# Turning half of the attention probabilities in 32x32 squares on VectorE and through DRAM, in a fused attention and feed-forward kernel

## The reference

```python
scores = jnp.einsum('bhnqd,bhnkd->bhnqk', qb, kwin) * scale
scores = jnp.where(mask[None, None], scores, jnp.float32(-1e+30))
attn = jax.nn.softmax(scores, axis=-1)
out = jnp.einsum('bhnqk,bhnkd->bhnqd', attn, vwin)
...
return out @ Wout + bout
```

## Time and profile before

| | |
|---|---|
| median of 3 runs | 2630.02 us (2627.89 to 2631.48) |
| profiled execution | 2629.41 us |
| its span | 2627.6 us |
| TensorE (PE) matmul, weight load | 98%, 80% of the span |
| VectorE (DVE), ScalarE (ACT), GpSimd (POOL) | 61%, 62%, 24% |
| DMA queues | 167.43 MB, mean 64 GB/s |

### The profile page before, as it was taken

The page is one execution under the profiler, slowest core; times in us unless marked ns, Lnnn a source line. Parts: engine busy times, 40 slices in busy tenths (PEclk is TensorE's granted clock), DMA queues, the critical chain, the costliest instruction groups (busy, mean ns, idle before and its releaser), DMA issues.

```text
span 2627.6 us, 55989 instructions
## 1 busy us (share of the span) xinstructions
PE 2576.2 (98%) x19728; PEld 2090.2 (80%) x19728; DVE 1592.0 (61%) x4779; ACT 1638.1 (62%) x4260; POOL 631.8 (24%) x595
## 2 busy tenths in 40 slices
PE   6999999999999999989999999999999999999998
PEld 4888888888888888868888888888888888888885
DVE  5444444444444444357777777777777777777775
ACT  6333333333333333358888888888888888888886
POOL 0011111111111111033333333333333333333332
PEclk7999999999999999999999999999999999999999
DMA  5422222222222222021121111112111111112110
GB/s 181 146 80 81 80 80 80 80 80 80 80 80 80 80 80 64 33 81 34 34 65 34 53 46 42 58 41 58 34 61 39 42 58 42 58 34 65 34 46 29
DMA packets 188361, 167.43 MB, mean 64 GB/s; under 512 B 11328, under 2 KB 143424, under 8 KB 187632
## 3 DMA queue, kind: packets, MB, share of 16 engines
q1 hardware_dynamic: 188000, 164.41, 20.2%
q0 software_dynamic: 144, 0.17, 0.0%
HBM read 97.43 MB, written 67.11 MB: 63 GB/s over the span
## 4 chain that ended last, share of the span: by engine, by line
PE 55%; ACT 1%; issue 0%; DVE 0%; POOL 0%; POOLq 0%; ACTq 0%
PE pT_ps L1193 14%; PE job_ps L1105 14%; PE score_ps L1176 7%; PE job_ps L1123 7%; PE job_ps L1217 7%; PE job_ps L1114 7%; ACT wqkv_raw L928 1%; ACT wqkv_raw L938 0%; PE job_ps L1237 0%; PE score_ps L1227 0%; DVE wqkv_raw L1006 0%; DVE k_lo L1038 0%; ACT q_hi L954 0%; ACT k_hi L957 0%; POOL wout_raw L899 0%
## 5 line engine op out<-in xcount | busy, mean ns | idle before, releaser
L928 ACT ACTIVATE wqkv_raw<-wqkv_raw,neg_max 128x384 f32<-128x384 f32 (+1 forms) x1024 | 633.3, 619 | 186.3 <-DVE neg_max L1006 181.5
L888 POOL TENSOR_SCALAR wqkv_raw<-wqkv_raw,sum_rcp 128x384 f32<-128x384 f32 (+1 forms) x256 | 372.9, 1457 | 960.1 <-DVE sum_rcp L1017 960.1
L494 ACT ACTIVATE relu<-up_ps,fc_scale 128x512 f32<-128x512 f32 x256 | 176.2, 688 | 656.2 <-PE up_ps L625 656.2
L938 ACT COPY wqkv_raw<-pT_ps 128x384 f32<-128x384 f32 (+1 forms) x1024 | 484.7, 474 | 74.4 <-PE pT_ps L1193 74.1
L1193 PE MATMUL pT_ps<-ident,wqkv_raw 128*128 128x128 f32 x3040 | 513.4, 277 | 8.1 <-ACT wqkv_raw L938 7.7
L1006 DVE CUSTOM_DVE_ANT_0 wqkv_raw<-score_ps,mask 128x384 f32<-128x384 f32 (+1 forms) x1024 | 503.5, 548 | 5.7 <-PE score_ps L1176 1.6
L568 DVE SCALAR_TENSOR_TENSOR sq<-up_ps,relu 128x512 f32<-128x512 f32 x256 | 177.0, 692 | 531.8 <-ACT relu L494 530.4
L1193 PEld LDWEIGHTS pT_ps<-ident,wqkv_raw 128*128 128x128 f32 x3040 | 360.0, 140 | 119.1 <-ACT wqkv_raw L938 42.6
L635 PE MATMUL down_ps<-proj_T,sq_hi 128*128 128x512 f32 x1024 | 408.9, 399 | 0.9 <-DVE sq_lo L551 0.9
L637 PE MATMUL down_ps<-proj_T,sq_lo 128*128 128x512 f32 x1024 | 404.3, 395 | 0.0
L621 PE MATMUL up_ps<-f_xT_hi,fc_T 128*128 128x512 f32 x1024 | 399.2, 390 | 1.4 <-DVE low L539 1.4
(11 more groups left out here) (126 smaller groups left out, 4228.2 us busy)
## 6 DMA issues: line engine op xcount, KB each, us to landing
xT_hi<-xT SPq DMA_DIRECT2D x65, 256.0 KB, 3.8
xT_lo<-xT SPq DMA_DIRECT2D x65, 256.0 KB, 4.5
f_x_in<-in_L_attn_x SPq DMA_DIRECT2D x64, 256.0 KB, 3.2
xT<-f_xT_hi SPq DMA_DIRECT2D x64, 256.0 KB, 2.6
xT<-f_xT_lo SPq DMA_DIRECT2D x64, 256.0 KB, 2.8
part_in<-in_L_attn_x SPq DMA_DIRECT2D x64, 256.0 KB, 3.4
partial<-f_y SPq DMA_DIRECT2D x64, 256.0 KB, 2.0
wout_raw<-partial SPq DMA_DIRECT2D x64, 256.0 KB, 2.8
```

The costliest lines, as they stand in the source:

```text
L888: nc.gpsimd.tensor_scalar(probs[:, u, cols], probs[:, u, cols], sum_rcp[:, u:u + 1], None, ALU.mult).then_inc(last_head_normalised, 1)
L928: nc.scalar.activation(probs[:, u, cols], probs[:, u, cols], ACT.Exp, bias=neg_max[:, u:u + 1], scale=-1.0, accum_out=prob_sum[:, u:u + 1] ...
L938: nc.scalar.copy(pT[:, h, first + seen.start:first + seen.stop, :].rearrange("p w t -> p (w t)"), pT_ps[:, h % 2, seen.start * P:seen.stop ...
```

## The change

Of the two query blocks of a step only block 1 is still turned by TensorE and copied by ScalarE. Block 0 takes another way. VectorE makes one reciprocal for its four heads; heads 0 and 1 are multiplied by ScalarE, head 2 by VectorE, head 3 by GpSimd. VectorE then transposes each head (128x384) in 32x32 squares, in the order 2, 0, 1, 3, into `blocks`. A square stays in its 32 partitions, so the squares must still be moved: SP stores the whole of `blocks` (128 partitions x 12 pieces of 512 B, 786 KB) to a DRAM tensor with one transfer, waits for it, and loads it with four transfers, each into 32 partitions of `pT_moved`. TensorE waits for these four (`blocks_moved`) ahead of the values of step t in step t + 1. These matmuls no longer join both blocks: there are 24 of 128 columns instead of 8 of 256 and 8 of 128. In return for space in SBUF `values` holds 5 blocks instead of 6 and the halves of the result 6 steps instead of 8. SP's list now goes by steps: transfers out and in first, then loads of x (c = 1), then y and `partial` (c = 2 and 3).

The core of the diff (the remaining lines are semaphores, changed counts in waits, and arguments):

```diff
-    VR = 6
+    VR = 5
     XR = 3
+    OR = 6
+    STRIPS = P // DH
...
-        pT = wqkv_raw[:, 2:4, :].rearrange("p a (h w k) -> p (a h) w k", w=6, k=P)
-        oT_hi = sb("oT_hi", [P, 2, DC, T], F32R)
-        oT_lo = sb("oT_lo", [P, 2, DC, T], F32R)
+        blocks = sb("blocks", [P, STRIPS, 3, HC, DH], F32)
+        pT_moved = wqkv_raw[:, 2, :].rearrange("p (w q h t) -> p w q h t", q=STRIPS, h=HC, t=DH)
+        pT = wqkv_raw[:, 3, :].rearrange("p (h w k) -> p h w k", w=3, k=P)
+        oT_hi = sb("oT_hi", [P, OR, T], F32R)
+        oT_lo = sb("oT_lo", [P, OR, T], F32R)
...
+        def transfers_out(steps):
+
+            return steps + (STRIPS - 1) * min(steps, DC)
...
+            def move_blocks_out(t):
+                i, _ = where(t)
+                first = blocks_seen(i, 0).start
+                moved = turned_dram[t % 2 * STRIPS:(t % 2 + 1) * STRIPS, :, :, :]
+                sp.wait_ge(blocks_turned, HC * (t + 1))
+                if first == 0:
+                    sp.dma_start(moved.rearrange("a w p x -> p (a w) x"),
+                                 blocks.rearrange("p a w h t -> p (a w) (h t)")).then_inc(blocks_out, 16)
+                else:
+                    for a in range(STRIPS):
+                        sp.dma_start(moved[a, first:3, :, :].rearrange("w p x -> p w x"),
+                                     blocks[:, a, first:3, :, :].rearrange("p w h t -> p w (h t)")).then_inc(blocks_out, 16)
+
+            def move_blocks_in(t):
+                i, _ = where(t)
+                first = blocks_seen(i, 0).start
+                sp.wait_ge(blocks_out, 16 * transfers_out(t + 1))
+                if t >= 1:
+                    sp.wait_ge(pv_done, t)
+                for a in range(STRIPS):
+                    moved = turned_dram[t % 2 * STRIPS + a, first:3, :, :].rearrange("w (q j) x -> j (w q) x", j=DH)
+                    sp.dma_start(pT_moved[a * DH:(a + 1) * DH, first:3, :, :, :].rearrange("j w q h t -> j (w q) (h t)"),
+                                 moved).then_inc(blocks_moved, 16)
...
-            for i in range(NT + 1):
-                if 1 <= i:
-                    for b in range(2):
-                        store_y(i - 1, b)
-                        if i < NT:
-                            load_part(i, b)
-                if i + XR - 1 < NT:
+            for t in range(STEPS + DC):
+                i, c = where(t)
+                if t < STEPS:
+                    move_blocks_out(t)
+                    move_blocks_in(t)
+                if c == 1 and i + XR - 1 < NT:
                     load_x(i + XR - 1)
+                if c >= 2 and i >= 1:
+                    store_y(i - 1, c - 2)
+                    if i < NT:
+                        load_part(i, c - 2)
...
+            def normalise_moved_head(t):
                 i, _ = where(t)
-                cols = window(i, b)
-                u = b * HC + HC - 1
-                pool.wait_ge(rcp_done, 2 * (2 * t + b) + 2)
+                cols = window(i, 0)
+                u = HC - 1
+                pool.wait_ge(rcp_done, 3 * t + 1)
...
+            def normalise_first_heads(t):
                 i, _ = where(t)
-                seen = blocks_seen(i, b)
-                first = 3 * at(i, b)
-                act.wait_ge(turned, 8 * t + b * HC + h + 1)
+                cols = window(i, 0)
+                act.wait_ge(rcp_done, 3 * t + 1)
+                for u in range(HC // 2):
+                    nc.scalar.mul(probs[:, u, cols], probs[:, u, cols], sum_rcp[:, u:u + 1]
+                                  ).then_inc(act_heads_normalised, 1)
...
+                    normalise_first_heads(t)
...
                     if h == 0 and 1 <= t <= STEPS:
                         oT_high(t - 1)
-                    if t < STEPS:
-                        copy_pT(t, 0, h)
...
+                if t >= 1 and b == 0:
+                    dve.wait_ge(blocks_turned, HC * t)
+                if t >= 1 and b == 1:
+                    dve.wait_ge(turned, HC * t)
...
+            def inverse_sums(t, first, count):
+                heads = slice(first, first + count)
+                dve.wait_ge(exped, 8 * t + first + count)
+                nc.vector.reciprocal(sum_rcp[:, heads], prob_sum[:, heads]).then_inc(rcp_done, 1)
...
+            def normalise_moved_head(t):
                 i, _ = where(t)
-                cols = window(i, b)
-                for pair in range(2):
-                    first = b * HC + 2 * pair
-                    heads = slice(first, first + 2)
-                    dve.wait_ge(exped, 8 * t + first + 2)
-                    nc.vector.reciprocal(sum_rcp[:, heads], prob_sum[:, heads]).then_inc(rcp_done, 1)
-                    dve.wait_ge(rcp_done, 2 * (2 * t + b) + pair + 1)
-                    for u in range(first, first + 2):
-                        if u % HC < HC - 1:
-                            nc.vector.tensor_scalar(probs[:, u, cols], probs[:, u, cols], sum_rcp[:, u:u + 1], None,
-                                                    ALU.mult).then_inc(normalised, 1)
+                cols = window(i, 0)
+                u = HC - 2
+                inverse_sums(t, 0, HC)
+                dve.wait_ge(rcp_done, 3 * t + 1)
+                nc.vector.tensor_scalar(probs[:, u, cols], probs[:, u, cols], sum_rcp[:, u:u + 1], None, ALU.mult
+                                        ).then_inc(dve_head_normalised, 1)
...
+            def turn_blocks(t, u):
+                i, _ = where(t)
+                seen = blocks_seen(i, 0)
+                if u < HC // 2:
+                    dve.wait_ge(act_heads_normalised, HC // 2 * t + u + 1)
+                elif u == HC - 2:
+                    dve.wait_ge(dve_head_normalised, t + 1)
+                    if t >= 1:
+                        dve.wait_ge(blocks_out, 16 * transfers_out(t))
+                else:
+                    dve.wait_ge(pool_head_normalised, t + 1)
+                nc.vector.transpose(blocks[:, :, seen.start:seen.stop, u, :].rearrange("p a w t -> p w a t"),
+                                    probs[:, u, seen.start * P:seen.stop * P].rearrange("p (w a t) -> p w a t", a=STRIPS, t=DH)
+                                    ).then_inc(blocks_turned, 1)
...
-                    normalise(t, 0)
+                    normalise_moved_head(t)
+                    for u in (2, 0, 1, 3):
+                        turn_blocks(t, u)
...
-                pe.wait_ge(pT_done, 8 * t + 2 * HC)
...
+                pe.wait_ge(blocks_moved, 16 * STRIPS * (t + 1))
+                pe.wait_ge(pT_done, HC * (t + 1))
+                for b in range(2):
+                    seen = blocks_seen(i, b)
+                    for w in seen:
+                        blk = 2 * i - 1 + b + w
+                        for h in range(HC):
+                            head = c * HC + h
+                            strip = slice(h * DH, (h + 1) * DH)
+                            cols = slice(at(i, b) * P, (at(i, b) + 1) * P)
+                            out_ = job_ps[strip, bank, cols].rearrange("p (q t) -> p q t", t=DH)
+                            p = pT[:, h, w, :].rearrange("p (q t) -> p q t", t=DH) if b else pT_moved[:, w, :, h, :]
+                            last = nc.tensor.matmul(out_, values[:, blk % VR, head * DH:(head + 1) * DH], p,
+                                                    start=(w == seen.start), stop=(w == seen.stop - 1),
+                                                    tile_position=(0, h * DH))
...
-                    if t < STEPS:
-                        turn_probs(t, 0, part)
                     run_b(t, part)
...
+    turned_dram = nc.dram_tensor("turned_blocks", [2 * (P // DH), 3, P, HC * DH], F32, kind="Internal").ap()
```

More of the change, by code:

```diff
@@ L659, in _, with attention_stage @@
                 down(NT - 1, s)
-def attention_stage(nc, loaded, xT_dram, partial, out):
+def attention_stage(nc, loaded, xT_dram, partial, turned_dram, out):
     NBLK = partial.shape[0] // P
@@ L1082, in _ @@
                 if t < STEPS:
-                    normalise(t, 1)
+                    for pair in range(2):
+                        normalise(t, pair)
             add_out(NT - 1, 1, B_NUMBER[STEPS + 2], b_bank(STEPS + 2))
```

87 lines of the change are left out of this document (46 added, 41 removed).

## The result

The changed kernel takes **2723.13 us** (median of 4 runs, 2720.24 to 2727.5) against 2628.95 us for the kernel before (4 runs, 2627.36 to 2631.48): a ratio of 1.0359, 95% interval 1.0341 to 1.0377. The profiled execution took 2727.5 us, its span 2725.6, 98.0 more than before's 2627.6.

The account below looks back on a forecast made before the run. Two coinciding limits, TensorE's sum and the VectorE-ScalarE loop (scores, search, exponentials, scales), bound the kernel. Steps lengthen from 11.44 to 11.97 us: +68 over 128 steps, +4 at the end, on 2630.0: 2702 us, range 2625 to 2860.

Parts of the forecast that it names:

- the plain case: Whole kernel: the forecast as it stands, steps of 11.97 us on average and 2702 us in total, chance 0.53.
- Two passes: VectorE's transposes: rival that each needs two passes, 4 x 0.48 us more, step 13.9, about 2950 us; chance 0.05.
- r+3.38: Second block's max search starts 3.38 us after r, the start of the reciprocal closing the first block's exponentials; 1.86 later than before.
- Tight, but not the bound: Path over TensorE's B job, scores and handover: reaches the next search at r+7.15, ahead of VectorE's +7.48.
- waits for nothing else: ScalarE in the kernel before: second-block exponentials run one after another, a 0.48 us PSUM copy between two, without other waits.
- Both end by r+2.1: ScalarE: the projection's two high halves, placed behind its two new scalings, end 2.1 us after the first block's reciprocal starts.
- 2 us of cover: Squares' way through DRAM: 9.8 us from last transpose to TensorE against 11.9 us allowed, so hidden by about 2 us.
- Just covered: SP queue: loads of x, once in four steps, delay the following block's way out by up to 2 us, still hidden.
- TensorE waiting for a DMA ahead of the values: TensorE ahead of the values' matmuls: a sign that would show the forecast wrong; no size given.
- no row of this stage shows one: TensorE's clock: a lower clock with TensorE idle 2 us a step would come on top; left out of the number.
- The round trip shows: Squares' way through DRAM: rival that it lengthens steps, decisive from 11.9 us; 2751 us at half return rate; chance 0.24.
- TensorE alone is the bound: Attention step: faster rival, step falls towards TensorE's 10.0 us, 2450 us, or 2540 for half of it; chance 0.11.

Follow-up runs that it names:

- experiment 4: Kernel before, first block's TensorE turns and ScalarE copies left out, nothing in their place (old data): 2480.48 us, ratio 0.9435.
- experiment 5: Kernel before, complete, with four unused VectorE transposes of 128x384 added ahead of the low halves: 2829.91 us, ratio 1.0762.
- Experiments 2: Changed kernel with one VectorE transpose a step in place of four, from step 5 (three heads read old squares): 2661.24 us, ratio 1.0118.
- 3: Changed kernel with one transpose a step from step 5, and ScalarE's projection high halves ahead of its two scalings: 2618.87 us, ratio 0.9963.
- Experiment 1: Changed kernel without both transfers of the squares and the waits on them (old data): 2732.29 us, ratio 1.0388.
- experiment 6: Changed kernel with five unused matmuls of 512 columns ahead of TensorE's wait for the squares: 2708.70 us, ratio 1.029.
- 9: Changed kernel, VectorE scaling and turning heads 0 and 1 during the other exponentials, no ScalarE scalings, last transpose behind the low halves: 2673.15 us, ratio 1.0165.
- experiment 12: Changed kernel with heads scaled and turned in pairs, plus the way out split into one transfer per pair, with longer pieces: 2587.45 us, ratio 0.9852.

## Why the prediction was right, and where it was off

**The sum.** Forecast 2702 with 0.53 for the plain case; measured 2723. The direction and the mechanism hold: taking 1.4 us from TensorE and four copies from ScalarE is worth 1.2 us a step (experiment 4), four transposes ahead of the low halves cost 1.54 on the kernel before (experiment 5) and 1.78 on that of experiment 4, and TensorE's sum does not set the step. In the steps with the add the loop over VectorE and ScalarE does, as read; in the others it runs through TensorE.

**The transposes.** 0.48 apart from the max search's pace; 0.47 measured. Two passes are refuted. The second search was put at r+3.38 and came at r+3.31. Exponentials without copies: forecast 0.62, measured 0.60. The values' 48 loads take 1.28 us where 32 took 1.24, so the 1.44 that I kept was right.

**The step.** Forecast 12.20 and 11.74, measured 12.09 and 11.94 to 11.98. The mean of 12.02 lies near the forecast's 11.97 by luck: it hides two errors of opposite sign. "Tight, but not the bound" failed for the path over B in steps without the add: there the next search starts at r+7.23, earlier than my +7.48, but ScalarE waits for the turns of the second block, which stand behind B and the scores. Its row there:

```profile
1734.42 0.48 ACT L992 COPY wqkv_raw<-pT_ps 128x384 f32<-128x384 f32 x1 [0.56 <-PE pT_ps L1278]
```

The next r is 4.70 behind the search in place of 4.26, so VectorE's early start is lost to TensorE. This is a step of the prediction that failed: "waits for nothing else", said of ScalarE. In the step that I followed, which has the add, such a wait lengthens nothing, and I took its 4.26 for both kinds. The step ahead of it, without the add, already showed the wait, and 4.69 from the search to the next r:

```profile
1711.54 0.48 ACT L938 COPY wqkv_raw<-pT_ps 128x384 f32<-128x384 f32 x1 [0.33 <-PE pT_ps L1193]
```

That the steps before are all 11.43 to 11.46, with the add or without, said the same.

**ScalarE's order.** "Both end by r+2.1" is what the trace shows, and I took it as harmless. It is, with four transposes. Experiments 2 and 3 show that it is the very next limit, 0.5 us behind: three transposes less gained 0.42 us a step of their 1.4 without moving the scalings.

**The round trip.** Forecast 9.8 and 2 us of cover; measured up to 9.7, 10.6, 11.4 and 11.8 in the four steps of a tile. Experiment 1 shows that regular steps lose nothing. "Just covered", said of the loads of x, is nearly so: they use the cover up, and two steps of the whole trace are 0.26 and 1.0 us longer by it alone. The way out is faster than forecast (4.1 for 4.6 us), the way back slower: from its first issue to the values 5.5 us in the quietest of the four steps and 7.6 in the worst, where I had 5.0.

The prediction named a sign of being wrong, "TensorE waiting for a DMA ahead of the values", and it came: 113.9 us of such waits, nearly half of TensorE's idle time. The sign was badly chosen. As long as the squares come within the 2 us that TensorE would wait for the low halves anyway, one wait only takes the place of the other; without transfers the regular steps are the same.

**The clock.** I had left this outside the number: "no row of this stage shows one". That was the term that was missed in the sum. The changed kernel has 2.2 us of idle TensorE a step, the trace before had none to show it on. Long steps cost 12.2 us, some 10 of them by the lower clock (my estimate: 12.2 less 1.3 in two steps at 1.00 and 0.4 of lateness in each of two others), and experiment 6 took 14 back. At the end the values wait 5.33 us and their loads too run slow:

```profile
2696.22 1.06 PEld L1300 LDWEIGHTS job_ps<-wqkv_raw,values 128*32 128x32 f32 x40 [0.96 <-issue]
...
2709.18 1.94 PEld L1300 LDWEIGHTS job_ps<-wqkv_raw,values 128*32 128x32 f32 x40 [5.33 <-issue]
```

Of the profiled execution's 98.1 us the forecast had 72. The other 26.1 are the long steps (12.2), the regular ones (73.9 for 68), the end (9.2 for 4) and the later start (2.8).

**The rivals.** "The round trip shows" is wrong for the regular step of this kernel. It fits the variants whose loop is shorter, 3 and 9; for 9 the shorter way out of experiment 12 bears it out. The 32 partitions may have a part in it, 0.7 us and not the 2.9 of half the rate. "TensorE alone is the bound" is refuted by its own idle time here, and for the kernel before by experiment 5.

## What to carry to other kernels

When two limits lie on each other, price the work that leaves one of them and the work that arrives on the other separately, each by its own run: here −1.2 and +1.54 us a step. Then don't add them up blindly: the change came to +0.58, because the same transposes cost 1.78 once the slack beside the other limit was gone and they waited for their input. Then look one place behind the new limit: ScalarE's order was 0.5 us behind it, the round trip 0.1 to 2 us, and taking three transposes away gained 0.42 us of 1.4 as long as that order stood. Work that waits for a batch (scale all heads, turn all heads, send all heads) is cheapest to take off the loop by splitting the batch: pairs and a transfer for each pair turned +3.6% into −1.5%.

## What the runs showed of the hardware

**An idle stretch of TensorE costs more than itself.** In a stage that ran at 1.00 before, the granted clock was 0.50 after waits of 2.72 and 2.57 us. It is no matter of the stretch's length alone: after 2.06 us it fell in one place and not in another, and after 3.19 us it did not. Where it falls, the work behind the wait takes up to twice as long for a few us (values' loads 2.36 for 1.28; B up to its scores 4.20 for 3.0). Taking one wait away can bring it on, by joining two idle pieces into one (14 long steps for 5, experiment 1).

**Issue time does not follow the bytes.** On one queue 768 KB from SBUF to DRAM in 1536 pieces take 0.38 us to issue, 192 KB from DRAM to 32 partitions 0.46, and 48 KB from SBUF to SBUF 0.68 to 0.77. Shape and kind changed together.

**A transpose in 32x32 squares** of 128x384 four-byte elements takes 0.55 us, 0.47 from one to the next: the pace of the max search on the same shape.
